# Attention phase: order of second-half values, scaled keys, gate and output row in a slot, and earlier loads of the first two rows

## The reference

```
q = l2norm(x @ Wq) / sqrt(16); k = l2norm(x @ Wk); v = x @ Wv; gate = x @ Wg
P = strict(k_beta @ k.T * L);  Ainv = inverse by (I + P)
v = Ainv @ v;  k_cumdecay = Ainv @ (k_beta * exp(g))
step over chunks:  v_new = v_i - kcd_i @ S
                   o_i = q_i * exp(g_i) @ S + attn @ v_new
                   S = S * exp(g_last) + (k_i * exp(g_last - g_i)).T @ v_new
o = o * rsqrt(mean(o * o) + 1e-5) * norm_w * silu(gate);  out = o @ Wo
```

## Time and profile before

| what | value |
|---|---|
| median of 3 runs | 1255.26 us (1250.27 to 1258.14) |
| the profiled execution, its own time | 1255.64 us |
| its span from first to last instruction | 1253.8 us |
| mean granted TensorE clock | 0.93 |
| busy over the span | PE 83%, DVE 73%, ACT 47%, POOL 32% |
| stage of the change | about 224 to 844 us of the span |

### The profile page before, as it was taken

How to read it: one execution, slowest core, us unless ns; L and a number is a source line. 1 busy time by engine, 2 the same in 40 slices (tenths; PEclk the granted TensorE clock), 3 DMA queues, 4 the chain that set the end, 5 groups by cost and what they waited for, 6 DMA issues and landing times. The chain is left out here.

```text
span 1253.8 us, 38504 instructions
## 1 busy us (share of the span) xinstructions
PE 1038.9 (83%) x15542; PEld 738.8 (59%) x15542; DVE 911.5 (73%) x2403; ACT 595.3 (47%) x1614; POOL 405.2 (32%) x580
## 2 busy tenths in 40 slices
PE   2999977676888888888888876669999798799978
PEld 2888854344555555555555554548888664255556
DVE  3877646268888888988888888527776435899953
ACT  2433245344676666766767764454333352201152
POOL 2666530311221212122212221115665347500055
PEclk9999988798989999999999987779999889899979
DMA  9000012254444444444444443100000023944012
GB/s 259 8 2 1 1 56 101 61 103 95 105 96 95 92 91 91 105 101 96 83 97 99 100 93 75 36 3 1 1 1 1 17 57 79 268 135 135 1 34 101
DMA packets 282624, 93.30 MB, mean 74 GB/s; under 512 B 208976, under 2 KB 275408, under 8 KB 282448
## 3 DMA queue, kind: packets, MB, share of 16 engines
q1 hardware_dynamic: 280848, 88.23, 30.0%
q10 hardware_dynamic: 1600, 2.62, 0.7%
HBM read 56.20 MB, written 30.41 MB: 69 GB/s over the span
## 5 line engine op out<-in xcount | busy, mean ns | idle before, releaser
L1764 DVE TENSOR_TENSOR delta_tmp<-delta_PR 128x130 f32<-128x130 f32 (+12 forms) x416 | 156.5, 376 | 9.1
L1761 DVE TENSOR_TENSOR delta_PR<-delta_PR,delta_tmp 128x130 f32<-128x130 f32 (+12 forms) x416 | 152.7, 367 | 9.4
L1615 ACT ACTIVATE delta_y<-psum 32x128 f32<-32x128 f32 x256 | 68.1, 266 | 82.9 <-PE psum L1450 80.7
L1854 POOL TENSOR_TENSOR delta_VK<-delta_QK,both_eg 128x256 f32<-128x256 f32 x32 | 20.9, 653 | 253.7 <-DVE delta_QK L1696 253.7
L1416 PE MATMUL psum<-delta_T,delta_pad 128*32 128x128 f32 x2048 | 81.5, 326 | 17.5 <-DMA delta_T<-inverse_scratch 17.4
L1416 PEld LDWEIGHTS psum<-delta_T,delta_pad 128*32 128x32 f32 x2048 | 69.5, 133 | 28.3 <-DMA delta_T<-inverse_scratch 22.4
L1360 PE MATMUL psum<-both_w_in,delta_xT 128*128 128x512 f32 x128 | 68.0, 656 | 20.2 <-DMA delta_xT<-turned_scratch 10.2
L1878 POOL TENSOR_TENSOR delta_S<-delta_E,delta_Bm 128x128 f32<-128x128 f32 x32 | 16.4, 514 | 205.2 <-issue 198.2
L1463 PEld LDWEIGHTS psum<-delta_y,delta_Kd 32*32 32x32 f32 x2048 | 23.3, 112 | 99.3 <-ACT delta_y L1615 99.3
L506 POOL TENSOR_TENSOR ffn_H<-ffn_hid,ffn_H 128x512 fp32r<-128x512 f32 x48 | 61.7, 1290 | 57.2 <-DVE ffn_H L472 57.2
L1631 ACT ACTIVATE delta_wide<-delta_S 32x128 f32<-32x128 f32 x256 | 78.1, 305 | 3.1
(11 more groups left out here) (282 smaller groups left out, 2599.0 us busy)
## 6 DMA issues: line engine op xcount, KB each, us to landing
within_scratch<-delta_PT SPq DMA_DIRECT2D x128, 64.0 KB, 1.9
delta_PR<-within_scratch SPq DMA_DIRECT2D x16, 512.0 KB, 4.3
inverse_scratch<-delta_PR SPq DMA_DIRECT2D x16, 512.0 KB, 3.3
delta_T<-inverse_scratch SPq DMA_DIRECT2D x128, 64.0 KB, 2.8
space_T<-taps_scratch SPq DMA_DIRECT2D x8, 1024.0 KB, 5.8
X<-taps_scratch SPq DMA_DIRECT2D x8, 1024.0 KB, 8.9
X<-in_x SPq DMA_DIRECT2D x32, 128.0 KB, 9.8
turned_scratch<-gates_XT SPq DMA_DIRECT2D x16, 256.0 KB, 2.3
```

Of the source, the lines that this page charges most:

```text
L1615: i = a.activation(dst, heads(bank[6][rows, half * P:(half + 1) * P]), ACT.Copy)
L1761: i = v.tensor_tensor(after, after, t3, ALU.add)
L1764: i = v.tensor_tensor(t3, column.to_broadcast([P, j, n_after]), row.to_broadcast([P, j, n_after]), ALU.mult)
```

## The change

In the slot loops of `delta`:

- ACT: keep_y of the second half goes ahead of keep_kq, root_qk and exp_decays. root_o goes from behind the first keep_y of the next slot (tile O) to the end of the slot, behind keep_o (tile Z).
- DVE: scale_qk goes ahead of keep_gate, three solve steps earlier than keep_gate now stands. keep_gate stands one solve step later than before. sum_o goes from the end of the slot to ahead of keep_within. scale_o goes from the head of the next slot to behind keep_attn.
- POOL: gate_o goes from behind fade_second of the next slot to behind kept_k, for tile Z.
- SP: the loads of x for tiles 0 and 1 are issued in `gates`, behind the writes of the turned rows and ahead of the taps' store. The buffers are those of `delta`.

```diff
+        made["gates"].xT = made["delta"].xT
...
+    for t in range(2):
+        turned_in(e, B, M.xT, S, t)
     taps_store(e, B, M, S)
...
+def turned_in(e, B, xT, S, t):
+
+    b = t // BLK
+    e.wait_ge(S.xt_out[b % 2], 32 * (b // 2 + 1))
+    src = bass.AP(tensor=B.xT_dram, offset=t * P, ap=[[NT * P, P], [P * NT * P, KD], [1, P]])
+    e.dma_start(xT[t % 2].rearrange("p (k n) -> p k n", k=KD), src).then_inc(S.p_in[t % 2], 16)
...
-    def turned_in(t):
+    def rows_in(t):
         if t >= 2:
             e.wait_ge(S.p_vg, t - 1)
...
+            turned_in(e, B, M.xT, S, t)
...
-    for n in range(-1, SLOTS):
-        at(turned_in, n + 1)
+    for n in range(SLOTS):
+        at(rows_in, n + 1)
...
         at(keep_y, Z, 0)
-        at(root_o, n - LAG_OUT)
         at(widen, Z, 0)
         at(squares, n)
+        at(keep_y, Z, 1)
         at(keep_kq, n - LAG_FORM)
         at(root_qk, n)
         at(exp_decays, n - LAG_FORM)
-        at(keep_y, Z, 1)
         at(widen, Z, 1)
...
         at(keep_o, Z)
+        at(root_o, Z)
...
-        at(scale_o, O)
         solve(n, 0, 1)
...
         at(new_state, Z, 1)
-        solve(n, 15, 18)
+        solve(n, 15, 16)
+        at(scale_qk, n)
+        solve(n, 16, 19)
         at(keep_gate, n)
-        solve(n, 18, 20)
-        at(scale_qk, n)
-        solve(n, 20, 23)
+        solve(n, 19, 22)
+        at(sum_o, Z)
+        solve(n, 22, 23)
         at(keep_within, n - LAG_FORM)
         solve(n, 23, 24)
         at(keep_attn, n - LAG_FORM)
-        solve(n, 24, 26)
+        solve(n, 24, 25)
+        at(scale_o, Z)
+        solve(n, 25, 26)
         at(add_o, O)
...
         solve(n, 27, 29)
-        at(sum_o, Z)
...
         at(fade_second, Z)
-        at(gate_o, O)
         at(decayed_k, n)
         at(kept_k, n)
+        at(gate_o, Z)
```

More of the change, by code:

```diff
@@ L1889, in delta_gpsimd @@
     for n in range(SLOTS):
-        Z, O = n - LAG_SCAN, n - LAG_OUT
+        Z = n - LAG_SCAN
         at(fade_first, Z)
```

## The result

The changed kernel took 1281.90 us (median; 1274.43 to 1286.20), the kernel before 1254.11 us beside it. The ratio is 1.0215 (95% interval 1.0157 to 1.0273): 28 us slower. The forecast was 1270, in a range of 1240 to 1288.

The account below looks back on a forecast made before the run. DVE was taken as the fullest engine (88% in slots 8 to 31), its work just covering a ring of four engines. 24 + 0.5 - 10.5 + 0 = +14 on a median of 1255.26 gave 1270 us, range 1240 to 1288.

Parts of the forecast that it names:

- the forecast's own band: The span of times given to the forecast case itself, 1263 to 1277 us, with a chance of 0.42.
- the clock rival: Half of the 24 slots run PE's outputs and `within` at the low clock: +15, 1285 us; chance 0.18.
- the ring: Work handed round four engines, keep_within to keep_within; after the change 17.75 us in even slots, 18.17 in odd ones.
- keys behind the second keep_y: Even slots: keep_kq behind the second keep_y on ACT makes DVE wait 1.7 us ahead of faded_q.
- scale_qk, a step and POOL ahead of the gate: DVE, faded_q to keep_gate: scale_qk, one more solve step and POOL's collision lengthen it from 3.86 to 5.18 us.
- The 0.62 ahead of scale_o: DVE's wait for ACT's root ahead of scale_o, removed in 25 slots, at most 15.5 us.
- The wait ahead of keep_within: DVE would wait about 0.8 us a slot ahead of keep_within, with fewer solve steps behind keep_gate.
- the start: Early loads (5.7 us) and keys scaled ahead of the gate in the first slots: 10.5 us gained together.
- +24.5 for slots 7 to 31: A loss of 2.0 us a pair over 12 pairs, 24 us, plus 0.5 for slot 7.
- the pair taken for before, 33.92: Length of the pair from slot 24 to 26 before the change, set against 35.92 us after it.
- The tail: Slots 32 to 39: about 2 us lost to late inverses, about 2 won in the last; sum 0, bounds -4 and +4.

Follow-up runs that it names:

- e4: The kernel before with only the early loads of x for tiles 0 and 1 added: 1248.70 us, ratio 0.9933.
- e6: The changed kernel with 12 more 128x128 matmuls for each tile, in apply ahead of its wait for the inverse: 1268.87 us.
- e10: The changed kernel without the loads of the inverse; apply multiplies by zeros: 1306.71 us.
- e3: The changed kernel with the second keep_y and keep_gate back in their old order; output row in one slot and early loads kept: 1250.51 us.
- e11: e3 without the loads of the inverse; apply multiplies by zeros: 1204.34 us.
- e1: The changed kernel with the second keep_y on ACT back behind exp_decays, so the keys are copied first: 1258.54 us.
- e2: The changed kernel with keep_gate back ahead of scale_qk on DVE: 1257.81 us.
- e12: The kernel before without the loads of the inverse; apply multiplies by zeros: 1244.26 us, ratio 0.9913.
- e13: e3 with QK scaled ahead of the gate in slots 0 to 3 alone and, in odd slots, the last solve steps first: 1232.48 us.
- e15: e3 with 12 extra 128x128 matmuls a slot: 1267.24 us.
- e14: e13 with 12 extra 128x128 matmuls a slot: 1263.66 us.

## Why the prediction was right, and where its sum was not

The measured 1281.90 lies in the stated range and on the forecast side. But it lies outside the forecast's own band of 1263 to 1277, near the 1285 of the clock rival, and that rival's mechanism is a large part of it. The ring was foreseen; that the range held is in part owed to it.

**Right: the ring.** Its length was worked out as 17.75 and 18.17 and is 17.6 and 17.94 where PE's clock is up (odd slots up to 19: 18.25). From keep_within to faded_q it is 9.11 in slot 28 and 9.32 in slot 27 (forecast 9.05 and 9.46), from there to keep_gate 5.12 in slot 27 (5.2). Its parts hold when undone one by one: keys behind the second keep_y 1.5 (forecast 1.7), scale_qk, a step and POOL ahead of the gate 1.2 (forecast 1.3). The 0.62 ahead of scale_o is gone. The wait ahead of keep_within is 0.74 to 0.87 (forecast 0.8). A further wait, ahead of sum_o (0.48 and 0.75), was not counted; it lies beside PE's outputs and within and adds nothing: keep_gate to keep_within is 3.50 (forecast 3.51).

**Right: the start.** Counted from the start of the phase, slot 7 comes 11.6 us earlier (forecast 10.5): 5.7 are the loads, as forecast. Slot 1 waited 1.19 instead of 2.86. e4, with the loads alone, has 7.6 of the 11.6.

**Wrong in size: +24.5 for slots 7 to 31.** Two things were mis-sized. First, the pair taken for before, 33.92, comes from slots 24 and 25, and half of the 24 slots are different. In slots 8 to 19 DVE has new_stats too. Before, where DVE's own work sets the pace, this makes a slot longer; the keep_within of slots 13 to 15, with new_stats between, and of slots 21 to 23, without:

```profile
430.29 0.76 DVE L1713 TENSOR_TENSOR delta_PT<-psum,delta_E 128x256 f32<-128x256 f32 x2 [0.68 <-PE psum L1400]
446.53 0.75 DVE L1713 TENSOR_TENSOR delta_PT<-psum,delta_E 128x256 f32<-128x256 f32 x2 [0.25 <-PE psum L1400]
...
449.57 0.42 DVE L311 BATCH_NORM_STATS2 ln_stats<-X 128x6 f32<-128x256 f32 x1
...
464.82 0.76 DVE L1713 TENSOR_TENSOR delta_PT<-psum,delta_E 128x256 f32<-128x256 f32 x2 [0.68 <-PE psum L1400]
...
569.78 0.76 DVE L1713 TENSOR_TENSOR delta_PT<-psum,delta_E 128x256 f32<-128x256 f32 x2 [0.68 <-PE psum L1400]
...
585.50 0.76 DVE L1713 TENSOR_TENSOR delta_PT<-psum,delta_E 128x256 f32<-128x256 f32 x2 [0.24 <-PE psum L1400]
...
603.39 0.76 DVE L1713 TENSOR_TENSOR delta_PT<-psum,delta_E 128x256 f32<-128x256 f32 x2 [0.68 <-PE psum L1400]
```

That is a pair of 34.53 with new_stats and one of 33.61 without. In the longer ring most of new_stats is hidden: 35.86 with, 35.53 without (e6). So the change costs 1.3 us a pair in slots 8 to 19 and 1.9 in slots 20 to 31, 6 x 1.33 + 6 x 1.92 = 19.5 instead of 24. Second, before had long slots of its own, with low-clock matmuls: by its undisturbed pairs it would have taken 5.2 us less in slots 8 to 31 than the 414.05 that it did. That is why the filled e6, which has hardly any such slots, is only 15.3 above it in slots 7 to 31.

**Wrong in size: the clock, counted as 0.** Over its own undisturbed pairs the changed kernel lost 450.6 - 428.3 = 22.3 us in slots 8 to 31, the kernel before 5.2: +17 for low clock and late inverse together. With PE kept busy, 467.58 - 446.66 = 20.9 us of the changed kernel go. These are estimates from one execution each, and the changed kernel's was the slowest of its four. The rival had the mechanism and the place (15 us) with a chance of 0.18, on the ground that so far only some slots showed it. But the prediction had itself worked out that PE would stand 3.8 us in each odd slot, where no wait ahead of apply or outputs was above 1.1 before. It should have been the first case. The rule cited there from the Trainium skill ("TensorE: Matmul & The Clock Gate", section "HAM oscillation — how this bites in real kernels"), on waits between bursts in each round of a loop, held: e10 has the drop in nearly every slot.

**Not counted: the late inverse.** A shorter way of PE to apply makes a transfer late that came in time. In the changed kernel it moves PE's idle time, and costs little by itself (2.1 with PE kept busy). In e3, with its short ring, it is the next limit, worth up to 46 us together with the low clock behind it (e11).

**The tail,** taken as 0 with bounds -4 to +4, cost 5.6 in slots 32 to 37. e4 has 2.3 of it, with the early loads alone. The rest comes with the output row in one slot: e1, e2 and e3, which keep that, have 92.4 to 93.3 whatever the order of keys and gate. It needs the late inverse, as the prediction said of sum_o: without the inverse's loads the new order is the shorter one, 79.69 (e10, e11) against 81.81 (e12).

By stretches of the two profiled executions the sum is -12.24 + 36.20 + 5.58 = +29.5, for a forecast of +14. A ring priced 5 us too high hid part of a clock priced 17 too low.

## What to carry to other kernels

When a sum is made per round, look whether the rounds differ: set the new round against the old one of the same kind, and check the sum against the mean. After each reordering list every wait of the engine that is now ahead, transfers too. Where the gap ahead of matmuls that others wait for grows in each round, as here from about 1 us to 3.3 and more, price these matmuls at the low clock (here 2.1 us a slot). Before a short ring is written off, look whether the next limit can be moved as well: e13, against the changed kernel, has keys and gate in their old order and six solve steps ahead of the rest, and turns +2.2% into -2.0%.

## What the runs showed of the hardware

Removing a wait made a kernel slower. Without the inverse's loads the changed kernel took 25 us more, since the idle time of PE gathered in one piece of 3.7 us ahead of outputs, and outputs and within ran at 1.08 and 3.63 us instead of 0.65 and 1.95. The granted clock in slots 7 to 31 was 0.84 instead of 0.93.

Work that nobody needs made it faster. 12 matmuls more a tile, 2.84 us each time, took 13 us off the changed kernel and 42 off e10. In the orders where PE waited for the gate at most 1.04 us in undisturbed slots (e3, e13) the same matmuls cost 17 us (e15) and 31 us (e14).
